# Moving a block's statistics, one score pass and the last key pieces at the start of an attention and experts kernel

## The reference

```python
x = x + tanh(g_xattn) * xattn(layernorm(x), ctx)     # one head, softmax over 6404 keys
x = x + tanh(g_ffn) * ffn(layernorm(x))              # top 2 of 8 experts, relu between W1 and W2

query = layernorm(x) @ Wq + bq;  key = ctx @ Wk + bk;  value = ctx @ Wv + bv
weights = softmax(query @ key.T / sqrt(128));  attended = weights @ value
```

## Time and profile before

| | us |
|---|---|
| median of three runs | 274.97 |
| the profiled execution, its span | 274.55, 272.8 |
| TensorE matmul busy (98% of the span) | 266.0 |
| VectorE busy (77%) | 210.5 |
| ScalarE busy (69%) | 186.8 |
| POOL busy (40%) | 109.3 |

### The profile page before, as it was taken

How to read it: one execution, slowest core, us unless ns; L and a number is a source line. 1 busy time by engine, 2 the same in 40 slices (tenths; PEclk the granted TensorE clock), 3 DMA queues, 4 the chain that set the end, 5 groups by cost and what they waited for, 6 DMA issues and landing times.

```text
span 272.8 us, 5070 instructions
## 1 busy us (share of the span) xinstructions
PE 266.0 (98%) x1662; PEld 245.4 (90%) x1662; DVE 210.5 (77%) x406; ACT 186.8 (69%) x338; POOL 109.3 (40%) x144
## 2 busy tenths in 40 slices
PE   7999999999999999999999999999999999999994
PEld 7677989999999999999889999999889998999993
DVE  4889977897486898789637478876688699467696
ACT  2997575445675556556577798888546664999990
POOL 3899993556800030000001553661025444355720
PEclk9999999999999999999999999999999999999999
DMA  6700020000099100000000222435301011313312
GB/s 191 275 2 0 0 82 0 2 1 2 0 248 338 42 0 2 0 1 2 1 0 2 77 77 79 117 126 145 106 15 37 24 32 35 91 58 73 86 53 81
DMA packets 18485, 17.08 MB, mean 63 GB/s; under 512 B 2410, under 2 KB 14940, under 8 KB 18460
## 3 DMA queue, kind: packets, MB, share of 16 engines
q1 hardware_dynamic: 17372, 15.31, 18.7%
q0 software_dynamic: 640, 1.31, 1.7%
q10 hardware_dynamic: 448, 0.14, 0.2%
HBM read 13.34 MB, written 3.42 MB: 61 GB/s over the span
## 4 chain that ended last, share of the span: by engine, by line
PE 87%; DVE 8%; DMA 2%; issue 1%; ACT 1%; SPq 1%; DVEq 0%
PE ps L1473 9%; PE ps L1499 9%; PE ps L1474 9%; PE ps L1500 9%; PE ps L1501 9%; PE ps L1475 9%; PE ps L1395 7%; PE ps L1600 4%; PE ps L1586 3%; DVE pmax L999 2%; DMA tok<-in_x_dram 2%; PE ps L1575 2%; PE ps L1625 2%; PE ps L1627 2%; PE ps L1626 2%; PE ps L1601 2%
## 5 line engine op out<-in xcount | busy, mean ns | idle before, releaser
L906 ACT ACTIVATE ex_hi<-ps 128x768 fp32r<-128x768 f32 (+1 forms) x78 | 56.9, 730 | 55.9 <-PE ps L1475 54.4
L1214 DVE TENSOR_TENSOR ex_lo<-ps,ex_hi 128x768 fp32r<-128x768 f32 (+1 forms) x66 | 58.4, 885 | 23.0 <-ACT ps L910 20.7
L999 DVE TENSOR_REDUCE pmax<-ps 128x1 f32<-128x512 f32 (+2 forms) x74 | 62.4, 874 | 10.3 <-PE ps L1395 9.5
L1499 PE MATMUL ps<-ex_hi,ctx_both 128*97 128x384 f32 (+1 forms) x153 | 49.7, 325 | 0.0
L910 ACT ACTIVATE ps<-ps 128x768 f32<-128x768 f32 (+1 forms) x66 | 49.7, 752 | 0.0
L1474 PE MATMUL ps<-q_lo,ctxT_hi 96*128 96x384 f32 (+1 forms) x153 | 49.0, 321 | 0.0
L1475 PE MATMUL ps<-q_hi,ctxT_lo 96*128 96x384 f32 (+1 forms) x153 | 48.6, 318 | 0.0
L1500 PE MATMUL ps<-ex_hi,ctx_both 128*96 128x384 f32 (+1 forms) x153 | 48.6, 318 | 0.0
L1501 PE MATMUL ps<-ex_lo,ctx_both 128*97 128x384 f32 (+1 forms) x153 | 48.6, 318 | 0.0
L1473 PE MATMUL ps<-q_hi,ctxT_hi 97*128 97x384 f32 (+1 forms) x126 | 42.3, 336 | 0.3 <-DVE ex_lo L1214 0.2
L1395 PE MATMUL ps<-ctxT_hi,q_hi 97*128 97x512 f32 (+1 forms) x104 | 34.3, 400 | 0.7 <-DVE pmax L999 0.4
(11 more groups left out here) (227 smaller groups left out, 545.2 us busy)
## 6 DMA issues: line engine op xcount, KB each, us to landing
raw<-in_ctx_dram SPq DMA_DIRECT2D x6, 384.0 KB, 6.1
w_raw<-in_L_ffn_W_dram SPq DMA_DIRECT2D x8, 256.0 KB, 3.9
raw<-in_L_ffn_W_dram SPq DMA_DIRECT2D x8, 256.0 KB, 6.3
raw<-in_L_ffn_b_dram SPq DMA_DIRECT2D x8, 256.0 KB
shared<-routing SPq DMA_DIRECT2D x8, 192.0 KB
x_slots<-shared SPq DMA_DIRECT2D x1, 1088.0 KB, 6.3
y_slots<-shared SPq DMA_DIRECT2D x17, 64.0 KB, 1.5
shared<-in_L_ffn_b_dram SPq DMA_DIRECT2D x1, 512.0 KB, 3.4
```

What stands on the lines that cost most here:

```text
L906: nc.scalar.activation(ex_pair(ex_hi, u % P_RING, js, n), scores, ACT.Exp)
L999: nc.vector.tensor_reduce(pmax[:, FIRST_TILE[ROUND_BLOCK[r]] + t, place:place + 1], max_home(s)[:, 0:w], AX.X, ALU.max).then_inc(max_reduc ...
L1214: nc.vector.tensor_tensor(ex_pair(ex_lo, u % P_RING, js, n), whole, ex_pair(ex_hi, u % P_RING, js, n).bitcast(F32), ALU.subtract).then_inc ...
L1499: nc.tensor.matmul(dst[0:CA, :], ch[:, j, :], hi, start=(j == first), stop=False)
```

## The change

Six edits, all ahead of unit 2 of block 0:

- **DMAs.** The rows of x of block 1 are issued ahead of all keys, those of block 2 behind all groups of keys, with a semaphore of their own (`x_last_in`). The first group of keys comes in two halves, window 0 (`ctx_first_in`) and window 1.
- **Warm-up.** `WARM_NORM` is 2 where it was 6.
- **Statistics.** Those of block 2 move on VectorE from ahead of `split_q(0)` to between `finish_max(0)` and `row_max(0)`.
- **First pass.** `score_for_max(0)` moves ahead of the turning of windows 2 and 3, which now stands between passes 0 and 1.
- **Windows 9 and 10** are turned behind `turn_max(0)`; all four last windows stand there.
- **Windows 11 and 12** are rounded on ScalarE and split on VectorE behind exponential 0 and `ex_lo` of unit 0. Before, ScalarE rounded both ahead of exponential 0, and VectorE split window 11 ahead of `ex_lo` of unit 0 and window 12 behind it.

```diff
--- before.py
+++ after.py
@@ -45,7 +45,7 @@
 W_RING = 2
 WARM_UP = 10
 WARM_FOLD = 4
-WARM_NORM = 6
+WARM_NORM = 2
 EPS = 1e-5
 
 
@@ -321,6 +321,9 @@
 
         small_in, x_in, w_consts_in = sem("small_in"), sem("x_in"), sem("w_consts_in")
         x_later_in = sem("x_later_in")
+
+        ctx_first_in = sem("ctx_first_in")
+        x_last_in = sem("x_last_in")
         ctx_in = [sem(f"ctx_in{g}") for g in range(NG)]
         w_in = [sem(f"w_in{r}") for r in range(W_SLOTS)]
         out_done = sem("out_done")
@@ -505,13 +508,16 @@
             sync.dma_start(tok[:, tiles(0), :], xv[:, tiles(0), :]).then_inc(x_in, 16)
             sync.dma_start(wk_sb[0:C, :], wk).then_inc(small_in, 16)
             sync.dma_start(wk_sb[C:CA, :], bk.rearrange("(a h) -> a h", a=1)).then_inc(small_in, 16)
+
+            sync.dma_start(tok[:, tiles(1), :], xv[:, tiles(1), :]).then_inc(x_later_in, 16)
             for g in range(NG):
                 js = group_chunks(g)
                 whole = min(js[-1] + 1, FULL)
+                if g == 0:
+                    sync.dma_start(raw[:, 0:WINDOW, :], ctxv[:, 0:WINDOW, :]).then_inc(ctx_first_in, 16)
+                    js = js[WINDOW:]
                 sync.dma_start(raw[:, js[0]:whole, :], ctxv[:, js[0]:whole, :]).then_inc(ctx_in[g], 16)
-                if g == 0:
-                    later = slice(BLOCK_TILES[0], NT)
-                    sync.dma_start(tok[:, later, :], xv[:, later, :]).then_inc(x_later_in, 16)
+            sync.dma_start(tok[:, tiles(2), :], xv[:, tiles(2), :]).then_inc(x_last_in, 16)
             sync.wait_ge(pad_zeroed, 1)
             sync.dma_start(raw[0:TAIL, FULL, :], ctx[0, FULL * P:NKEY, :]).then_inc(ctx_in[NG - 1], 16)
             sync.dma_start(wv_sb[0:C, 0:HID], wv).then_inc(w_consts_in, 16)
@@ -641,6 +647,8 @@
             def split_ctx(g):
                 js = group_chunks(g)
                 hi = ch[:, js[0]:js[-1] + 1, 0:C]
+                if g == 0:
+                    pool.wait_ge(ctx_first_in, 16)
                 pool.wait_ge(ctx_in[g], 16 if js[-1] < FULL else 32)
                 nc.gpsimd.tensor_copy(hi, raw[:, js[0]:js[-1] + 1, :]).then_inc(ctx_hi_ready, 1)
                 pool.wait_ge(ctx_hi_ready, g + 1)
@@ -828,7 +836,7 @@
             copy_ctxT_hi(TURNED_BY_VECTOR - 1)
             copy_ctxT_whole(TURNED_BY_VECTOR - 1)
             copy_x(1)
-            for w in range(TURNED_BY_VECTOR, NW):
+            for w in range(TURNED_BY_VECTOR, NW - 2):
                 copy_ctxT_hi(w)
 
             def beside_first_block(i):
@@ -908,6 +916,10 @@
                         act.wait_ge(ctxT_lo_ready, TURNED_BY_VECTOR)
                     whole = ex_whole(u, js, n) if u in POOL_LO else scores
                     nc.scalar.activation(whole, scores, ACT.Exp).then_inc(ex_ready, 1)
+                    if u == 0:
+
+                        for w in range(NW - 2, NW):
+                            copy_ctxT_hi(w)
                     if b:
                         post(b - 1, i)
                     else:
@@ -1034,13 +1046,15 @@
             last.then_inc(first_norm, 1)
             dve.wait_ge(x_later_in, 16)
             statistics(0, 1)
-            statistics(0, 2)
             split_q(0)
             for s in range(SLOTS_UNTIL[0]):
                 reduce_max(s)
             finish_max(0)
+
+            dve.wait_ge(x_last_in, 16)
+            statistics(0, 2)
             row_max(0)
-            for w in range(TURNED_BY_VECTOR, NW - 1):
+            for w in range(TURNED_BY_VECTOR, NW - 2):
                 split_window(w)
 
             def post(b, i):
@@ -1223,7 +1237,8 @@
                         if b == NB - 1 and i == SPLIT_2.get(e):
                             split_second(e)
                     if b == 0 and i == 0:
-                        split_window(NW - 1)
+                        for w in range(NW - 2, NW):
+                            split_window(w)
                     if b == 0 and i == SECOND_ROW_UNIT - 2:
                         finish_max(1)
                     if b + 1 < NB and i == MAX_UNIT:
@@ -1347,7 +1362,10 @@
             def turn_window(w):
 
                 js = window_chunks(w)
-                pe.wait_ge(ctx_in[js[0] // NATURAL_GROUP], 16 if js[-1] < FULL else 32)
+                if w == 0:
+                    pe.wait_ge(ctx_first_in, 16)
+                else:
+                    pe.wait_ge(ctx_in[js[0] // NATURAL_GROUP], 16 if js[-1] < FULL else 32)
                 if 4 <= w < TURNED_BY_VECTOR:
                     pe.wait_ge(ctxT_f_ready, w - 3)
                 elif w >= TURNED_BY_VECTOR + 2:
@@ -1413,21 +1431,18 @@
             turn_window(0)
             turn_window(1)
             make_qk(0)
-            for w in range(2, 4):
-                turn_window(w)
+
             for s in range(SLOTS_UNTIL[0]):
                 score_for_max(s)
-                w = 4 + s
-                if s % 2 and w < TURNED_BY_VECTOR:
+                w = 3 if s == 0 else 4 + s
+                if (s == 0 or s % 2) and w < TURNED_BY_VECTOR:
                     turn_window(w - 1)
                     turn_window(w)
             turn_window(TURNED_BY_VECTOR - 1)
             pe.wait_ge(ctxT_f_ready, TURNED_BY_VECTOR - 3)
             turn_x(0, 1, x_home(1))
-            for w in range(TURNED_BY_VECTOR, NW - 2):
-                turn_window(w)
             turn_max(0)
-            for w in range(NW - 2, NW):
+            for w in range(TURNED_BY_VECTOR, NW):
                 turn_window(w)
 
             def beside_first_block(i):
```

## The result

The changed kernel takes 276.42 us (median of 6 runs, 276.35 to 276.48) against 274.98 us of the kernel before (6 runs, 274.61 to 275.20): 1.0053 times as long, 95% interval [1.0041, 1.0066]. It is slower, by 1.44 us where 1.24 was forecast. Its profiled execution took 276.43 us, with a span of 274.7, so the two traces lie 1.9 us apart; the execution of before that was profiled (274.55) was one of its shortest. The granted clock is 1.00 in every stretch of both up to 240 us; from there to the end it is 0.96 before and 1.00 now.

The account below looks back on a forecast made before the run. TensorE holds 87% of the chain of waits, VectorE 8%, so the start of TensorE's unit 4 was priced: -0.22 (T) + 0.84 (eight transposes) + 0.62 (split) = +1.24 us, forecast 276.2 us, range 275.3 to 277.0.

Parts of the forecast that it names:

- Order of landing: DMA queue: block 1's rows land at 5.9, first window 6.4, second 6.9, next key group 7.8 us.
- rival B: Second key window lands late, at 7.34, or the clock falls: +1.7, 276.7 us; chance 0.10.
- The pass: First score pass: reduction 0 starts at 9.38, 0.65 earlier, but 0.43 is lost to transposes between passes.
- T: Moment the last of VectorE's six maximum reductions is done: 16.9 before, forecast 16.7, 0.2 earlier.
- From T to unit 0: Wait before TensorE's first score unit: eight more transposes add 0.84, so unit 0 starts at T + 2.34, 19.05.
- VectorE's detour: VectorE before unit 0: block 2's statistics (1.18) then the row (0.43), ready at T + 1.9, hidden by the transposes.
- The split: VectorE between units 0 and 4: one more split of 512 columns, +0.62; up to 1.04 if ScalarE's copies decide.
- The sum: All terms together: +1.24 us on the profiled 274.55, forecast median 276.2; slower with chance 0.81.
- A: TensorE's other work at units 3 and 4 hides the split: +0.62, 275.6 us; chance 0.15.
- C: VectorE the only pole, unit 4 1.18 earlier, 273.8 us; faster only if its holes sum under 2.4; chance 0.06.
- D: No difference: T 0.95 earlier and half the split hidden, or tail holes absorb the loss; +0.2, 275.2; chance 0.11.

Follow-up runs that it names:

- h_pool_waits: Changed kernel with POOL's subtraction of the first key group waiting until VectorE has written block 2's variances: 276.10 us, 1.0037.
- i_pool_waits_windows: h_pool_waits with windows 9 and 10 turned ahead of the row of maxima again: 275.49 us, 1.0021.
- j_three: Changed kernel with the 128x3 last step of block 2's statistics written as three 128x1 instructions, POOL left running: 276.55 us, 1.0055.
- c_splits: Changed kernel with windows 11 and 12 rounded and split where they were before the change: 275.86 us, 1.0018.
- g_best3: Changed kernel with first pass, windows 9 and 10, roundings and splits of 11 and 12 as before, block 2's statistics moved to unit 3: 275.88 us, 1.0028.
- a_op: Changed kernel with the last step of block 2's statistics as a SCALAR_TENSOR_TENSOR instead of a TENSOR_SCALAR: 276.46 us, 1.0062.
- e_pool_halves: Changed kernel with POOL's subtraction of the first key group cut into two instructions of 128x384: 276.55 us, 1.0042.
- d_op_windows: a_op with windows 9 and 10 turned ahead of the row of maxima again: 276.40 us, 1.0044.
- k_pass: i_pool_waits_windows with the first score pass back behind windows 2 and 3: 276.46 us, 1.0025.
- l_rest_old: Changed kernel keeping only landing order, shorter warm-up and block 2's statistics place, with POOL's wait of h_pool_waits: 275.61 us, 1.0008.
- n_sum: Changed kernel with POOL's wait, windows 9 and 10 turned ahead, windows 11 and 12 as before, moved first pass kept: 274.73 us, 0.9986.

## Why the prediction was right

The sign and the size came out, and the mechanism in all but one term: TensorE's start of unit 4 sets the time, and it is late by VectorE's work and by what stands ahead of unit 0. What holds unit 0 was named wrongly. By its steps:

- **Order of landing, right.** Forecast landings 5.9, 6.4, 6.9 and 7.8; measured 2.1 + 3.6 = 5.7, 2.5 + 3.8 = 6.3, 2.9 + 3.8 = 6.7 and 3.4 + 4.3 = 7.7. Each half of 192 KB takes 3.8 us from its issue, where the whole of 384 KB took 4.3. The second lands at 6.7, 0.3 behind the whole of before but 0.2 ahead of the forecast, so rival B's second window (7.34) was not late. The row of the second half:

```profile
L519 SPq DMA_DIRECT2D raw<-in_ctx_dram x1: 432/432/432, 2.9 to 2.9; - x1
DMA to landing us min/median/max: 3.8/3.8/3.8
```

- **The pass, right.** First reduction 9.32 (9.38), holes between the first reductions (six take 7.31, not 6.87: 0.44 where I had 0.43), T 16.63 (16.7). In its parts: q_hi is 0.34 earlier, where I said 0.2, and the order costs 8.67 - 8.60 = 0.07.
- **From T to unit 0, mis-sized, and on the wrong engine.** Forecast T + 2.34; measured T + 3.00. "VectorE's detour is shorter ... ready at T + 1.9" is the sentence that failed. It priced the statistics by the rows of before, where POOL was in no long instruction: at 8.43 it was idle, waiting for that very step, and at 9.56 its instruction ended 0.05 later. Here POOL was in its subtraction, and the step took 1.15 longer. The row came at T + 2.94, not T + 1.9 (it is T + 1.80 in h and i, where POOL waits). As the transposes would have held unit 0 to T + 2.38 anyway (h), the stall costs 3.00 - 2.38 = 0.62. I had looked at POOL, found it busy for 9.91 of 10 us, and passed it over because no TensorE instruction waits for it. VectorE does, without a semaphore. The Trainium skill (SBUF — State Buffer, "Who interferes with whom") says it: VectorE's second pair of ports is GpSimd's only one; an instruction of VectorE in a mode with two ports, or one with two inputs in SBUF beside a GpSimd instruction that reads SBUF, and a GpSimd instruction exclude one another for the whole of the one that came first. The traces agree: 1.32 us for either form, 0.71 beside the memset. The Trainium skill (VectorE: DVE Perf Modes, "Mode 2×_2P") has such a mode for one source in SBUF whose outermost dimension that isn't 1 is even or equal in source and result. 128x3 falls under it, 128x1 has no such dimension; the trace agrees with 0.28 us for three in j_three.
- **The split, right.** 0.62 forecast, 0.60 measured at unit 4, 0.56 in the median (c_splits). ScalarE's copies did not decide. Unit 4 less unit 0 is 7.50, as forecast.
- **The sum.** Forecast -0.22 + 0.84 + 0.62 = +1.24. Measured at unit 4: -0.27 (T) + 0.87 (transposes and what they hide of the statistics: 2.38 less the 1.51 of before) + 0.62 (stall) + 0.62 (split and rounding) = +1.84. The median moved by only 1.44, for the median of before lies 0.43 above its profiled execution and that of the changed kernel does not. Of the two errors, 0.6 too little at unit 0 and 0.4 too much in what the median shows, most cancel. That the time came out near the forecast is in part luck.
- **Rivals.** A (the split hidden) falls by c_splits. C (VectorE as the only pole, faster) falls: VectorE stood for 0.95 + 0.38 + 0.44 + 0.88 = 2.65 us, more than C's 2.4, and was stalled for 0.54 and 1.15 more. D needed T 0.95 earlier, and it came 0.27 earlier; even g_best3, with 0.86 at T, lost it at unit 6. B was wrong in the landing, and the granted clock of the changed kernel never fell.

**Why the changed kernel's runs lie so close together** (over 0.13 us, those of before over 0.59 beside them and over 2.2 in 35 later runs): unit 0 is held by POOL's subtraction, which starts when POOL's earlier work is done: at 17.34 to 17.40 in six traces (the changed kernel, a, e, c, d and j), with T anywhere from 16.55 to 17.42. With an early T VectorE waits longer (1.32 in the changed kernel, 1.10 in c_splits, where T is 0.2 later), and the end is the same, 19.1. The runs agree as far as they go: they spread over 0.25 us in c_splits and 0.33 in d_op_windows, which keep the stall (and a_op, but for its three), and over 1.2 in h_pool_waits, 0.8 in i_pool_waits_windows and 1.7 in e_pool_halves, which don't or not always. That T varies in the runs that nobody traced is not shown.

**Open** is why the second group lands anywhere from 7.5 to 9.4, and whether this is what spreads the runs of before, of which only one was traced. That k_pass and l_rest_old, which have its order, spread by 1.8 and 2.4 us speaks for it; n_sum, which doesn't, spreads by 0.7 but for one run at 276.28. Against it, g_best3 has its order too and spreads by 1.2, and e_pool_halves spreads by 1.7 without it. The landing of the rows of x and the pace of TensorE's first instructions, below, are candidates as well.

## What to carry to other kernels

An instruction's duration read from one place holds at another only if the neighbours are the same: when a VectorE step moves into a stretch where GpSimd is busy, look at its form and at what GpSimd does there, even if no semaphore joins them. When two delays end in the same wait, take both away before you call either harmless. And a pass put ahead of work that hangs on a DMA costs where the data is early and saves where it is late. Here, by the distances above, it costs 8.67 - 8.25 = 0.42 us with the keys at 7.5 and, as an estimate, saves 17.90 - (8.16 + 8.67) = 1.07 with them at 9.4. So judge it by many runs, not by one trace.

## What the runs showed of the hardware

- A VectorE step of 128x3 elements, from SBUF to SBUF, took 0.17 us alone and up to 1.32 beside a GpSimd (POOL) instruction, then always ending within 0.05 us of it. A GpSimd memset, which only writes, held it as well (0.71). The TENSOR_SCALAR of 128x1 did not wait (three in 0.28), nor did the three BATCH_NORM_AGGREGATE of 128x6 (0.32).
- TensorE's first instructions come at two paces, at a granted clock of 1.00 in the profile: its weight loads start 0.21 us apart at first and 0.11 apart later. The moment of the step differs between executions, from about 4.9 us in n_sum and a_op to about 7.6 in e_pool_halves. The turn of the norm and the eight transposes of windows 0 and 1, in h_pool_waits, where the step comes at 7.3:

```profile
6.01 0.44 PEld L1388 LDWEIGHTS ps<-ident,norm 128*128 128x128 f32 x2
6.43 1.32 PEld L1379 LDWEIGHTS ps<-ident,raw 128*96 128x96 f32 x8
```

  and in i_pool_waits_windows, where it comes at 5.4 and the transposes wait for the keys instead:

```profile
5.85 0.20 PEld L1388 LDWEIGHTS ps<-ident,norm 128*128 128x128 f32 x2
6.31 0.91 PEld L1379 LDWEIGHTS ps<-ident,raw 128*96 128x96 f32 x8 [0.26 <-DMA raw<-in_ctx_dram]
```

  q_hi is 0.56 us later in the first (8.56 against 8.00), and so is T. In the four traces with the step at 7.0 or later (e, h, j, l) q_hi is at 8.53 to 8.73, in all others with the shorter warm-up at 8.16 or earlier. What sets the moment I can't say from these runs: it differs between executions whose work on TensorE up to there is the same. Half a microsecond of an execution can come from it, which is as much as some edits here were worth.
